# A gated two-layer transformer block on one core: the low parts of the second attention's logits as 64-row products, two batches side by side

## The reference, cut to what matters

```python
def _L1_xattn_ref(x, init, Wq, bq, Wk, bk, Wv, bv):      # x, init: [16, 64, 512]
    q = jnp.einsum('dc,bct->btd', Wq, init) + bq          # DQK = 64
    k = jnp.einsum('dc,bct->bdt', Wk, init) + bk[None, :, None]
    R = jnp.einsum('btd,bds->bts', q, k)                  # per batch [512, 512]
    attention = jax.nn.softmax(R, axis=-1)
    v = jnp.einsum('oc,bct->bto', Wv, x) + bv
    return jnp.einsum('bts,bsc->bct', attention, v)
# x = x + tanh(g_xattn[0]) * L0_xattn(layernorm(x), ctx)   32 query heads, 8 key heads
# x = x + tanh(g_ffn[0])   * L0_ffn(layernorm(x))          4-bit weights, 8-bit activations
# x = x + tanh(g_xattn[1]) * L1_xattn(layernorm(x), ctx)
# x = x + tanh(g_ffn[1])   * L1_ffn(layernorm(x))          base matrix and four experts of rank 8
```

## Time and profile before

| | |
|---|---|
| median of three runs | 795.96 us |
| profiled execution, whole | 795.32 us |
| its span (first to last instruction) | 793.5 us |
| TensorE products busy | 780.8 us (98%), 4940 instructions |
| TensorE weight loads busy | 638.8 us (81%) |
| VectorE, ScalarE, GpSimd busy | 541.4, 437.7, 498.0 us |
| granted TensorE clock | 1.00 over the span |

### The profile page before, as it was taken

The page is one execution under the profiler, slowest core; times in us unless marked ns, Lnnn a source line. Parts: engine busy times, 40 slices in busy tenths (PEclk is TensorE's granted clock), DMA queues, the critical chain, the costliest instruction groups (busy, mean ns, idle before and its releaser), DMA issues.

```text
span 793.5 us, 13550 instructions
## 1 busy us (share of the span) xinstructions
PE 780.8 (98%) x4940; PEld 638.8 (81%) x4957; DVE 541.4 (68%) x1043; ACT 437.7 (55%) x824; POOL 498.0 (63%) x430
## 2 busy tenths in 40 slices
PE   8999999999999999999999999999999999999998
PEld 7888888888888888888888888888765777777776
DVE  6857866666676545466655555555899987998874
ACT  5754455444454434444454433333579898888773
POOL 2797477645556764475676456546457885887753
PEclk9999999999999999999999999999999999999999
DMA  9312533432523131952113111267273413213101
GB/s 335 107 66 68 139 80 81 133 97 72 148 77 89 40 102 58 47 147 77 63 40 105 43 51 27 36 64 277 82 191 95 107 48 81 74 49 80 48 16 40
DMA packets 77778, 71.02 MB, mean 89 GB/s; under 512 B 51552, under 2 KB 52800, under 8 KB 77328
## 3 DMA queue, kind: packets, MB, share of 16 engines
q1 hardware_dynamic: 77424, 69.82, 34.1%
q10 hardware_dynamic: 288, 0.33, 0.1%
HBM read 49.04 MB, written 6.34 MB: 70 GB/s over the span
## 4 chain that ended last, share of the span: by engine, by line
PE 87%; DVE 4%; DMA 4%; POOL 2%; ACT 2%; issue 1%; another core or an unknown queue 1%; SPq 0%; DVEq 0%
PE bank L81 11%; PE bank L83 10%; PE bank L82 10%; PE bank L554 7%; PE bank L577 6%; PE bank L572 6%; PE bank L573 6%; PE bank L667 4%; PE bank L1645 4%; PE bank L1631 3%; PE bank L1597 2%; PE bank L1568 2%; PE bank L1576 2%; PE bank L1621 2%; DMA w_out<-w_quant 2%; PE bank L1622 2%
## 5 line engine op out<-in xcount | busy, mean ns | idle before, releaser
L970 DVE SCALAR_TENSOR_TENSOR x_res<-bank,gate,x_res 128x512 f32<-128x512 f32 x128 | 95.4, 747 | 74.0 <-PE bank L577 73.4
L1231 POOL TENSOR_TENSOR prob<-prob,row_inv 128x512 f32<-128x512 f32 x32 | 33.4, 1044 | 166.1 <-DVE row_inv L966 159.5
L1217 POOL TENSOR_TENSOR rope_swap<-rope_swap,trig 128x512 f32<-128x512 f32 x80 | 104.0, 1300 | 30.6 <-ACT rope_swap L737 30.3
L736 ACT COPY rope_swap<-bank 64x512 f32<-64x512 f32 x80 | 46.7, 584 | 110.3 <-DVE rope_cos L941 110.2
L941 DVE TENSOR_TENSOR rope_cos<-bank,trig 128x512 f32<-128x512 f32 x80 | 54.2, 678 | 76.5 <-PE bank L83 71.4
L572 PE MATMUL bank<-wo_hi,oT_hi 128*128 128x512 f32 x256 | 101.7, 397 | 1.2 <-DVE x_res L970 0.6
L81 PE MATMUL bank<-xnT_hi,wq_hi 128*128 128x512 f32 x252 | 101.5, 403 | 0.0
L573 PE MATMUL bank<-wo_lo,oT_hi 128*128 128x512 f32 x256 | 100.8, 394 | 0.0
L83 PE MATMUL bank<-xnT_hi,wq_lo 128*128 128x512 f32 x252 | 99.9, 396 | 0.0
L82 PE MATMUL bank<-xnT_lo,wq_hi 128*128 128x512 f32 x252 | 99.5, 395 | 0.0
L1223 POOL TENSOR_TENSOR q_rope<-rope_cos,rope_swap 128x512 f32<-128x512 f32 x64 | 84.2, 1315 | 5.0
(11 more groups left out here) (273 smaller groups left out, 1936.2 us busy)
## 6 DMA issues: line engine op xcount, KB each, us to landing
wq_raw<-in_wq_tiles SPq DMA_DIRECT2D x16, 512.0 KB, 3.8
wo_raw<-in_L_xattn_wo SPq DMA_DIRECT2D x16, 512.0 KB, 3.9
xn<-in_L_ffn_Wd SPq DMA_DIRECT2D x16, 256.0 KB, 3.6
b_ctx<-in_ctx SPq DMA_DIRECT2D x32, 128.0 KB, 2.6
b_k_twice<-b_qk_hi SPq DMA_DIRECT2D x32, 128.0 KB, 2.4
w_T_dram<-w_out SPq DMA_DIRECT2D x28, 128.0 KB, 3.1
w_T<-w_T_dram SPq DMA_DIRECT2D x2, 1376.0 KB, 19.9
xn<-in_L_ffn_Wg SPq DMA_DIRECT2D x10, 256.0 KB, 3.0
```

The costliest lines, as they stand in the source:

```text
L970: dve.scalar_tensor_tensor(out=K.x[:, t, :], in0=wo_ps[t % 2][:, :], scalar=K.gate[:, 0:1], in1=K.x[:, t, :], op0=ALU.mult, op1=ALU.add).t ...
L1217: pool.tensor_tensor(out=sw, in0=sw, in1=sin_b, op=ALU.mult).then_inc(s_rope, 1)
```

## The change

- `k_lo` is two buffers, [i], in place of four. The low key of the even batch lies in rows 0 to 63, that of the odd batch in rows 64 to 127; nothing is left to be zero. The four memsets, their semaphore and the wait for it go; the sync queue waits for `s_av` at that place.
- `q_stack` of the odd batch is turned over: its high query lies in the upper rows 64 to 127, its low query in the lower ones. (`k_twice` has the same content in both halves.)
- The low product contracts only the 64 rows of its own parity, for all 64 pieces: form 64\*128 in place of 128\*128.
- `two_logits(t, n)` issues four products: high of n, high of n + 1, low of n, low of n + 1. 24 such fours take the place of 48 single calls; 16 calls stay single.
- 11 of the 24 neighbours stood next to each other in TensorE's list before. For the other 13, one of the two moves: for instance logits(0, 4) moves up past up_mm(0, 2) and x_transpose(1), logits(1, 7) down past up_mm(2, 2), logits(3, 0) down past weights_T(2, 4) and qk(4, 1), logits(3, 3) up past qk(5, 0), two value products, three transposes, logits(3, 4) down past gate_mm(4, 0), logits(3, 5) up past qk(5, 1), logits(4, 6) down past weights_T(4, 2) and qk(6, 0), logits(4, 7) up past h_transpose_a(4) and weights_T(4, 3). The lists of the other engines stay.

```diff
@@ sync queue @@
-            sp.wait_ge(M.s_k_zero, 4)
+            sp.wait_ge(s_av, 2 * NPAIR)
@@ GpSimd, end of the first part @@
-            pool.wait_ge(s_av, 2 * NPAIR)
-            for i in range(2):
-                for par in range(2):
-                    pool.memset(f32(M.k_lo[i][par][:, :]), 0.0).then_inc(M.s_k_zero, 1)
@@ buffers @@
-    M.q_stack, M.k_lo, M.k_twice = ([two(f"b_{n}{i}", [P, D], F32R) for i in range(2)] for n in ("q_stack", "k_lo", "k_twice"))
+    M.k_lo = two("b_k_lo", [P, D], F32R)
+    M.q_stack, M.k_twice = ([two(f"b_{n}{i}", [P, D], F32R) for i in range(2)] for n in ("q_stack", "k_twice"))
@@ def duplicate_tile @@
-    for dst, src in ((M.q_stack[i][par][lower, :], M.qk_hi[par][lower, :]),
-                     (M.q_stack[i][par][upper, :], M.qk_lo[par][lower, :]),
+    own, other = (lower, upper) if par == 0 else (upper, lower)
+    for dst, src in ((M.q_stack[i][par][own, :], M.qk_hi[par][lower, :]),
+                     (M.q_stack[i][par][other, :], M.qk_lo[par][lower, :]),
                      (M.k_twice[i][par][lower, :], M.qk_hi[par][upper, :]),
                      (M.k_twice[i][par][upper, :], M.qk_hi[par][upper, :]),
-                     (M.k_lo[i][par][lower, :], M.qk_lo[par][upper, :])):
+                     (M.k_lo[i][own, :], M.qk_lo[par][upper, :])):
@@ TensorE @@
-            def logits(t, n):
+            def logits_high(t, n):
...
                 pe.matmul(r_ps[par][:, :], q, k_twice[t % 2][par][:, :], start=True, stop=False)
-                pe.matmul(r_ps[par][:, :], q, k_lo[t % 2][par][:, :], start=False, stop=True).then_inc(s_r, 1)
+
+            def logits_low(t, n):
+                tb, par = n // 2, n % 2
+                ch = slice(par * S, (par + 1) * S)
+                pe.matmul(r_ps[par][:, :], q_stack[t % 2][par][ch, tb * P:(tb + 1) * P], k_lo[t % 2][ch, :], start=False, stop=True
+                          ).then_inc(s_r, 1)
+
+            def logits(t, n):
+                logits_high(t, n)
+                logits_low(t, n)
+
+            def two_logits(t, n):
+                nxt = (t, n + 1) if n < NB - 1 else (t + 1, 0)
+                logits_high(t, n)
+                logits_high(*nxt)
+                logits_low(t, n)
+                logits_low(*nxt)
@@ TensorE's list, one of 24 places @@
-            logits(3, 3)
             weights_T(3, 0)
             low(1)
-            logits(3, 4)
             pe.wait_ge(s_hTa_sb, 4)
             gate_mm(4, 0)
+            two_logits(3, 4)
             pe.wait_ge(s_xT_sb, 5)
             qk(5, 1)
-            logits(3, 5)
             weights_T(3, 1)
             pe.wait_ge(s_gate, 13)
             down(3)
```

More of the change, by code:

```diff
@@ L1721, in tensor @@
             up_mm(0, 1)
-            logits(0, 1)
-            logits(0, 2)
+            two_logits(0, 1)
             pe.wait_ge(s_gate, 2)
@@ L1726, in tensor @@
             first.low_T((2, 3))
-            logits(0, 3)
+            two_logits(0, 3)
             pe.wait_ge(s_up, 2)
@@ L1731, in tensor @@
             x_transpose(1)
-            logits(0, 4)
             weights_T(0, 0)
@@ L1743, in tensor @@
             gate_mm(1, 1)
-            logits(0, 6)
-            logits(0, 7)
+            two_logits(0, 6)
             weights_T(0, 2)
@@ L1751, in tensor @@
             up_mm(1, 1)
-            logits(1, 0)
+            two_logits(1, 0)
             weights_T(0, 4)
-            logits(1, 1)
             pe.wait_ge(s_up, 5)
@@ L1767, in tensor @@
             x_transpose(2)
-            logits(1, 2)
+            two_logits(1, 2)
             weights_T(0, 6)
-            logits(1, 3)
             pe.wait_ge(s_out, 1)
@@ L1799, in tensor @@
             gate_mm(2, 2)
-            logits(1, 7)
             pe.wait_ge(s_hTb_sb, 2)
             up_mm(2, 2)
+            two_logits(1, 7)
             weights_T(1, 3)
-            logits(2, 0)
             pe.wait_ge(s_gate, 9)
@@ L1818, in tensor @@
             weights_T(1, 6)
-            logits(2, 2)
-            logits(2, 3)
+            two_logits(2, 2)
             pe.wait_ge(s_xT_sb, 4)
@@ L1831, in tensor @@
             qk(4, 0)
-            logits(2, 4)
+            two_logits(2, 4)
             weights_T(2, 0)
@@ L1836, in tensor @@
             h_transpose_a(2)
-            logits(2, 5)
             pe.wait_ge(s_hTb_sb, 3)
@@ L1842, in tensor @@
             down(2)
-            logits(2, 6)
+            two_logits(2, 6)
             weights_T(2, 2)
-            logits(2, 7)
             pe.wait_ge(s_out, 3)
@@ L1850, in tensor @@
             up_mm(3, 2)
-            logits(3, 0)
             weights_T(2, 4)
@@ L1854, in tensor @@
             qk(4, 1)
-            logits(3, 1)
+            two_logits(3, 0)
             weights_T(2, 5)
@@ L1863, in tensor @@
             x3_T(1)
-            logits(3, 2)
+            two_logits(3, 2)
             pe.wait_ge(s_v, 3)
@@ L1889, in tensor @@
             up_mm(4, 0)
-            logits(3, 6)
-            logits(3, 7)
+            two_logits(3, 6)
             z_T(1)
@@ L1898, in tensor @@
             weights_T(3, 4)
-            logits(4, 0)
-            logits(4, 1)
+            two_logits(4, 0)
             weights_T(3, 5)
@@ L1910, in tensor @@
             x_transpose(5)
-            logits(4, 3)
-            logits(4, 4)
+            two_logits(4, 3)
             pe.wait_ge(s_xT_sb, 6)
@@ L1930, in tensor @@
             h_transpose_b(4)
-            logits(4, 6)
             weights_T(4, 2)
@@ L1934, in tensor @@
             qk(6, 0)
+            two_logits(4, 6)
             pe.wait_ge(s_gate, 17)
@@ L1937, in tensor @@
             weights_T(4, 3)
-            logits(4, 7)
             pe.wait_ge(s_hTb_sb, 5)
@@ L1952, in tensor @@
             up_mm(5, 2)
-            logits(5, 1)
-            logits(5, 2)
+            two_logits(5, 1)
             weights_T(4, 6)
@@ L1962, in tensor @@
             weights_T(4, 7)
-            logits(5, 3)
-            logits(5, 4)
+            two_logits(5, 3)
             pe.wait_ge(s_v, 5)
@@ L1992, in tensor @@
             weights_T(5, 4)
-            logits(6, 0)
-            logits(6, 1)
+            two_logits(6, 0)
             weights_T(5, 5)
@@ L2002, in tensor @@
             x_transpose(7)
-            logits(6, 2)
-            logits(6, 3)
+            two_logits(6, 2)
             weights_T(5, 6)
@@ L2022, in tensor @@
             up_mm(7, 1)
-            logits(6, 4)
+            two_logits(6, 4)
             weights_T(6, 1)
-            logits(6, 5)
             base(3)
@@ L2031, in tensor @@
             h_transpose_b(6)
-            logits(6, 6)
+            two_logits(6, 6)
             weights_T(6, 2)
@@ L2036, in tensor @@
             gate_mm(7, 2)
-            logits(6, 7)
             pe.wait_ge(s_hTb_sb, 7)
@@ L2047, in tensor @@
             weights_T(6, 5)
-            logits(7, 1)
-            logits(7, 2)
+            two_logits(7, 1)
             weights_T(6, 6)
@@ L2068, in tensor @@
             h_transpose_a(7)
-            logits(7, 5)
+            two_logits(7, 5)
             weights_T(7, 2)
-            logits(7, 6)
             pe.wait_ge(s_hTa_sb, 8)
```

1 line of the change is left out of this document (removed).

## The result

The changed kernel takes 804.69 us (median of six, 803.17 to 806.5), the kernel before beside it 795.67 (median of six): ratio 1.0115, interval 1.0102 to 1.0129. So it is slower by 9.0 us, where I had forecast 7.6. The profiled execution took 804.67 us, with a span of 802.9.

What follows compares the result with a forecast made beforehand. TensorE was taken to bound the kernel, nearly wholly in the last 210 us. Fours +2.7, singles +5.3, absorbed -0.5, order +0.6, zeroing -0.5 made +7.6 us, from the median 803.6 us, range 797 to 810.

Steps and rivals of the forecast that it cites:

- The mechanism: TensorE's low products: each form edge costs a 0.10 us pause and an exposed load; fours +2.7 us, singles +5.3 us.
- The order: 13 of 24 fours moved: VectorE gets some low products later, clearest at (3,4), down(3) late by about 0.5; +0.6 us.
- The bound of 3: Upper bound, in us, on the cost of the moved logits, forecast at +0.6 with bounds 0 and 3.
- Absorbed: TensorE's existing waits at 602.41 and 774.19 swallow part of the added cost: -0.5 us, bounds 0 and -1.4.
- The wait at 602: TensorE's 0.84 us wait at 602.41 for VectorE and ScalarE work; 0.2 us each of (0,6) and (1,0) vanish there.
- The 0.53 at the end: TensorE's 0.53 us wait at 774.19, taken to leave a little air for absorbing added cost.
- The zeroing: GpSimd's four memsets from 571.28 hold VectorE's 16x128 copy and so delay TensorE's L577; removing them gives -0.5 us.
- The sync queue's earlier loads and two buffers for four: Next context loads start up to 2 us earlier, DMAs as many and as large as before; cost nothing.
- would have made the pack a gain: TensorE's fours: lows side by side, no pause, loads pulled ahead; -5.6 us, near 790.5 us, chance 0.12.
- rival 3: Edges are paid but TensorE's hidden short waits take 6.4 of the 8.0 us: 797.2, chance 0.08.
- rival 2: In the fours, the 512-column lows don't stream side by side: +12.7, near 808.7 us, chance 0.12.
- rival 4: VectorE comes late once for each of the 13 moved fours, 6.5 us: 809.5, chance 0.08.

Runs made afterwards that it cites:

- order-only kernel: The changed kernel's new order with its 24 fours, but low products of 128 rows and the data and memsets of before: 1.0046 to before.
- the first experiment: All 64 low products in the 64-row form in the order of before, none paired, nothing zeroed: 815.39 us, 1.0234 to before.
- same-rows kernel: The changed kernel, but both low products of a four use rows 0 to 63, so they cannot stream side by side: 1.0178 to before.

## Why the prediction was right, point by point

- **The mechanism** was right as forecast: lows side by side, loads late by a product and the pause, the next load exposed as well. Beside the order-only kernel, a single costs 0.28, 0.35 or 0.38 us (bf16, transposes, f32 behind it; forecast 0.29, 0.33, 0.38) and a four 0.06, 0.11 or 0.17 (forecast 0.065, 0.107, 0.157). Over 24 fours and 16 singles that is 2.8 + 5.3 = 8.1 us, forecast 8.0. (16 fours are followed by transposes and 5 by f32 products, not 15 and 6: z_T behind (3,6) is transposes. It changes the sum by 0.05.) The block of L667, the same form in the first part of the kernel, gave the pause and the f32 load. The two shorter loads were an estimate, 0.083 us off the length of each record, and the prices with them came out within 0.02.
- **The order** was the mis-sized term: 0.6 forecast, 2.3 measured. At (3,4) down(3) waits 0.35 where 0.5 was forecast, right in kind. But "the bank waits of the logits moved up have the exponentials just finished" failed in three of the moved fours, where 1.2 us of load waits stand, and the stretch around (2,6), which the forecast doesn't name, alone costs 1.1 us. The bound of 3 held.
- **Absorbed**: what is left over is 8.1 + 2.3 - 9.7 = 0.7, forecast 0.5. The wait at 602 is 0.43 us in the change and was 0.93 in the order-only kernel. The cost of the singles (4,5) and (7,3) is absorbed as well, some 0.7 us together, but a new wait of 0.32 for f_h stands at 641.98. The 0.53 at the end stayed. So the place was right for 0.5 us, and that the rest nearly cancels is luck.
- **The zeroing**: 0.54 us in these two profiles, forecast 0.5. The path was as forecast, the copy held and the subtractions only queued behind it. Not foreseen: the hold isn't the same in each execution, in one profile it cost nothing.
- **The sync queue's earlier loads and two buffers for four** cost nothing, as forecast: no TensorE wait after 580 us names a DMA.
- The sum: 8.1 + 2.3 - 0.7 = 9.7 in part two (the 0.7 is what remains, so this closes by itself), less the 0.54 of the zeroing: 9.2, for a measured 9.0.
- **Rivals**: the page of the Trainium skill "TensorE: Matmul & The Clock Gate", section "Part 3: Packing small matmuls — row/col tiling", would have made the pack a gain. Its side by side streaming is what the trace shows (the two lows start 3 to 4 ns apart); that there is no edge is not, 0.31 us of empty load path in front of each. Here the measurement decides. Slack (rival 3) fell with the first experiment, "lows don't stream together" (rival 2) with the same-rows kernel. The order (rival 4) was real, at a third of its price.

## What to carry to other kernels

Before packing half-height products into a stream of full ones, find a place in the trace where the two forms meet and read both edges: here 0.10 us of pause each way and a weight load that is no longer hidden. A pack of two saves one product (0.23 us) and its two edges cost more, 0.29 to 0.40 by what comes next. By these numbers two packs in a row (0.46 saved) would just pay; that is an estimate, and no run here has such a run of packs. And moving work next to its neighbour in a full list moves its buffer's deadline too: read the consumer's waits at each place moved.

## What was new of the hardware

- An edge between forms costs the pause (0.10 us) also where the products are tiny (16 rows, 4 columns), and there it is all that it costs.
- Within a run of one form the loads are hidden, also where two 64-row products use the same rows: the second starts 0.34 us after the first, of which 0.11 is the first one's own load (same-rows kernel, 711.87 and 712.21).
- Not every height makes an edge. The 96-row product of `down` (L1597, trace of before) follows a 128-row one in 0.22 us, the usual step of these bf16 products.
- A copy of 16x128 from SBUF to SBUF took 1.96, 1.50 and 1.03 us beside the memsets in three profiles, and 0.22 without them, while two subtractions of 128x512 with one input from PSUM took 1.29 us beside the memsets, as without them.
